# Gated product kept in PSUM and split from there; GpSimd's weight split runs without waiting for VectorE

## The reference

```
h = layernorm(x) * (1 + cb) + sb                      # 2048 x 128
probs = sigmoid(h @ router_w.T + expert_bias)          # 160 experts
top 8 of each token, normalised and scaled by 2.5 -> combine (2048 x 160)
h1 = silu(einsum('th,eih->eti', h, w_gate))            # every expert, 64 inner features
routed = einsum('eti,ehi->th', h1 * combine.T[:, :, None], w_down)
shared = silu(h @ w_gate_shared.T) @ w_down_shared.T
x = x + gb * (routed + shared)
```

## Time and profile before

| | |
|---|---|
| median of 3 runs | 525.52 us (522.47 to 527.17) |
| profiled execution | 521.39 us, span 519.6 us |
| PE busy | 495.6 us, 95% of the span |
| DVE busy | 431.3 us, 83% |
| ACT busy | 392.2 us, 75% |
| POOL busy | 150.6 us, 29% |
| DMA | 110.15 MB, mean 212 GB/s |

### The profile page before, as it was taken

One profiled execution on the slowest core, in us unless ns is written; L12 is line 12 of the kernel. 1 busy time (PEld: TensorE's weight loads), 2 busy tenths in 40 slices (PEclk: granted clock), 3 DMA queues, 4 the chain that ended last, 5 costly groups with the idle time before them and its releaser, 6 DMA issues.

```text
span 519.6 us, 7819 instructions
## 1 busy us (share of the span) xinstructions
PE 495.6 (95%) x2159; PEld 396.0 (76%) x2159; DVE 431.3 (83%) x513; ACT 392.2 (75%) x440; POOL 150.6 (29%) x144
## 2 busy tenths in 40 slices
PE   7686699999999999999999999999999999999996
PEld 5475488777787788888888788788888888888885
DVE  5999888787878788787888797887878888788886
ACT  3267687787878787888888787878878787878873
POOL 3787434222222222222222222222222222222210
PEclk9699899999999999999999999999999999999999
DMA  7000899999999999999999999999999999999962
GB/s 240 1 1 8 216 226 265 227 225 226 234 227 233 242 236 240 230 235 239 230 239 231 221 241 233 232 245 234 237 236 239 242 239 244 233 239 231 225 176 81
DMA packets 38934, 110.15 MB, mean 212 GB/s; under 512 B 6564, under 2 KB 10788, under 8 KB 38920
## 3 DMA queue, kind: packets, MB, share of 16 engines
q1 hardware_dynamic: 38596, 109.32, 88.5%
q10 hardware_dynamic: 324, 0.67, 0.4%
HBM read 107.58 MB, written 2.38 MB: 212 GB/s over the span
## 4 chain that ended last, share of the span: by engine, by line
PE 74%; DMA 13%; DVE 8%; SPq 2%; issue 1%; ACT 1%; POOL 0%; DVEq 0%
PE ps L921 37%; PE ps L906 37%; DMA cb<-combine_scratch 10%; DVE gu L722 2%; DMA combine_scratch<-combT_b 1%; DMA x_sb<-x 1%; DVE stT L686 1%; SPq L280 1%; DVE picked L715 1%; DVE bn L600 1%; DVE picked L703 0%; PE ps L860 0%; DVE mod_gate L659 0%; DVE xn L615 0%; DVE top L698 0%
## 5 line engine op out<-in xcount | busy, mean ns | idle before, releaser
L722 DVE TENSOR_TENSOR gu<-ps,cb 128x1024 f32<-128x1024 f32 x161 | 196.7, 1222 | 76.8 <-DMA cb<-combine_scratch 69.3
L509 ACT ACTIVATE ps<-ps 128x1024 f32<-128x1024 f32 x161 | 162.1, 1008 | 62.8 <-PE ps L906 60.1
L729 DVE TENSOR_TENSOR g_lo<-gu,g_hi 128x1024 fp32r<-128x1024 f32 x162 | 199.8, 1233 | 0.1
L522 ACT ACTIVATE g_hi<-gu 128x1024 fp32r<-128x1024 f32 x162 | 170.9, 1055 | 29.2 <-DVE gu L722 24.7
L404 POOL TENSOR_TENSOR w_lo<-w_raw,w_hi 128x384 fp32r<-128x384 f32 x98 | 99.7, 1017 | 312.1 <-DVE g_lo L729 312.1
L906 PE MATMUL ps<-h_hi,w_hi 128*128 128x512 f32 x324 | 103.8, 401 | 4.1 <-DVE gu L722 1.7
L906 PE MATMUL ps<-h_hi,w_lo 128*128 128x512 f32 x324 | 102.1, 396 | 0.0
L906 PE MATMUL ps<-h_lo,w_hi 128*128 128x512 f32 x324 | 102.1, 396 | 0.0
L921 PE MATMUL ps<-g_lo,w_hi 128*128 128x512 f32 x324 | 100.6, 392 | 1.5 <-DVE g_lo L729 1.5
L921 PE MATMUL ps<-g_hi,w_hi 128*128 128x512 f32 x324 | 101.1, 393 | 0.0
L921 PE MATMUL ps<-g_hi,w_lo 128*128 128x512 f32 x324 | 101.0, 392 | 0.0
(11 more groups left out here) (99 smaller groups left out, 206.9 us busy)
## 6 DMA issues: line engine op xcount, KB each, us to landing
cb<-combine_scratch SPq DMA_DIRECT2D x322, 256.0 KB, 5.1
w_raw<-experts SPq DMA_DIRECT2D x54, 384.0 KB, 7.0
x_sb<-x SPq DMA_DIRECT2D x4, 256.0 KB, 4.9
out<-xn SPq DMA_DIRECT2D x3, 256.0 KB, 2.2
combine_scratch<-combT_a ACTq DMA_DIRECT2D x1, 512.0 KB, 5.5
wmod_sb<-wmod SPq DMA_DIRECT2D x1, 384.0 KB, 3.5
combine_scratch<-combT_a SPq DMA_DIRECT2D x1, 384.0 KB, 3.1
proj_sb<-proj SPq DMA_DIRECT2D x1, 272.0 KB, 4.9
```

The lines of the kernel that those rows point to most:

```text
L509: act.activation(slot(z), slot(z), ACT.Silu).then_inc(silu_done, 1)
L522: act.activation(g_hi[:, k % RING, :], gu[:, k % RING, :], ACT.Copy).then_inc(hi_ready, 1)
L722: dve.tensor_tensor(gu[:, k % RING, :].rearrange("p (b n) -> p b n", b=2), slot(z), cb[:, k % RING, :].rearrange("p (b n) -> p b n", b=2), ...
L729: dve.tensor_tensor(g_lo[:, k % RING, :], gu[:, k % RING, :], g_hi[:, k % RING, :].bitcast(F32), ALU.subtract).then_inc(lo_ready, 1)
```

## The change

gu is gone. The gate writes its product back to the PSUM slot that it reads; hi and lo read the slot. The shared expert's sigmoid, which stood in gu, now stands in cb's first buffer. Since lo is now the last reader of a slot, PE's waits before it overwrites a slot are for lo instead of the gate, in the opening and in the loops. The gate's wait for lo(j-3) is gone. POOL's two halves of w_lo no longer wait for lo.

```diff
                 pool.wait_ge(w_hi_ready, group - FIRST_GROUPS + 1)
-                pair = WG * (group - 2) + 1
                 half = WG * P
                 for n in range(2):
-                    pool.wait_ge(lo_ready, pair + n + 1)
                     cols = slice(n * half, (n + 1) * half)
...
-            def gated_hi(j, k):
+            def gated_hi(j, z, k):
                 act.wait_ge(gated, j + 1)
                 if not (isinstance(j, int) and j < RING):
                     act.wait_ge(down_done, j - RING + 1)
-                act.activation(g_hi[:, k % RING, :], gu[:, k % RING, :], ACT.Copy).then_inc(hi_ready, 1)
+                act.activation(g_hi[:, k % RING, :].rearrange("p (b n) -> p b n", b=2), slot(z), ACT.Copy
+                               ).then_inc(hi_ready, 1)
...
             def gate(j, z, k):
                 dve.wait_ge(silu_done, j + 1)
-                if not (isinstance(j, int) and j < RING):
-                    dve.wait_ge(lo_ready, j - RING + 1)
-                dve.tensor_tensor(gu[:, k % RING, :].rearrange("p (b n) -> p b n", b=2), slot(z),
-                                  cb[:, k % RING, :].rearrange("p (b n) -> p b n", b=2),
+                dve.tensor_tensor(slot(z), slot(z), cb[:, k % RING, :].rearrange("p (b n) -> p b n", b=2),
                                   ALU.mult).then_inc(gated, 1)
...
-            def gated_lo(j, k):
+            def gated_lo(j, z, k):
 
                 dve.wait_ge(hi_ready, j + 1)
-                dve.tensor_tensor(g_lo[:, k % RING, :], gu[:, k % RING, :], g_hi[:, k % RING, :].bitcast(F32),
+                dve.tensor_tensor(g_lo[:, k % RING, :].rearrange("p (b n) -> p b n", b=2), slot(z),
+                                  g_hi[:, k % RING, :].bitcast(F32).rearrange("p (b n) -> p b n", b=2),
                                   ALU.subtract).then_inc(lo_ready, 1)
...
                 users = [p for p in range(j) if FIRST_SLOTS[p] == z]
                 if users:
-                    pe.wait_ge(gated, users[-1] + 1)
+                    pe.wait_ge(lo_ready, users[-1] + 1)
...
                 j = PAIRS * c + BODY * i + k
-                pe.wait_ge(gated, j + 1)
+                pe.wait_ge(lo_ready, j + 1)
                 if ahead % WG == 0:
                     pe.wait_ge(w_split, WGROUPS * c + WG * i + ahead // WG + 1)
```

More of the change, by code:

```diff
@@ L148, in adaln_layer @@
         w_lo = sb("w_lo", [P, RING, 2 * WG * P], F32R)
-        gu = sb("gu", [P, RING, CHUNK])
         g_hi = sb("g_hi", [P, RING, CHUNK], F32R)
@@ L514, in shared_sigmoid @@
                 act.wait_ge(z_ready, 1)
-                act.activation(gu[:, 0, :].rearrange("p (b n) -> p b n", b=2), slot(FIRST_SLOTS[0]), ACT.Sigmoid
+                act.activation(cb[:, 0, :].rearrange("p (b n) -> p b n", b=2), slot(FIRST_SLOTS[0]), ACT.Sigmoid
                                ).then_inc(silu_done, 1)
-            def gated_hi(j, k):
+            def gated_hi(j, z, k):
                 act.wait_ge(gated, j + 1)
@@ L546, in first_hi @@
             def first_hi(j):
-                gated_hi(j, j)
+                gated_hi(j, FIRST_SLOTS[j], j)
             for stage, n in (
@@ L568, in turn @@
                         silu(j + 1, (k + 1) % RING)
-                    gated_hi(j, k)
+                    gated_hi(j, k % RING, k)
                     if k % WG == 1 and not (last and c == CHUNKS - 1 and k > 1):
@@ L734, in shared_gate @@
                 dve.wait_ge(silu_done, 1)
-                both = gu[:, 0, :].rearrange("p (b n) -> p b n", b=2)
-                dve.tensor_tensor(both, slot(FIRST_SLOTS[0]), both, ALU.mult).then_inc(gated, 1)
+                z = slot(FIRST_SLOTS[0])
+                dve.tensor_tensor(z, z, cb[:, 0, :].rearrange("p (b n) -> p b n", b=2), ALU.mult).then_inc(gated, 1)
             def first_gate(j):
@@ L742, in first_lo @@
             def first_lo(j):
-                gated_lo(j, j)
+                gated_lo(j, FIRST_SLOTS[j], j)
             for stage, n in (
@@ L767, in turn @@
                         gate(j + 1, ahead % RING, ahead)
-                    gated_lo(j, k)
+                    gated_lo(j, k % RING, k)
             for c in range(CHUNKS):
```

## The result

| | before | after |
|---|---|---|
| median | 526.35 us (4 runs, 522.47 to 529.44) | 541.76 us (4 runs, 538.88 to 542.84) |
| ratio | | 1.029, 95% interval 1.021 to 1.037 |
| profiled execution, span | 521.39, 519.6 | 542.84, 541.0 |

The change makes the kernel 15.4 us slower by the medians. A ratio leaves out runs that lie over 1.5% above the fastest run of their kernel; a median keeps them. The two profiled executions lie 21.45 us apart: the one of before is shorter than its four runs in the table, and the one of after is the longest of its four. Sizes read from the pair of profiles therefore add up to some 6 us more than the medians show.

The account below looks back on a forecast made before the run. PE was taken as full at 2.78 us a pair, with DMA's limit almost coinciding. 12.95 + 1.4 + 1.4 = +15.7 us on the profiled 521.4 gave 537.1, plus 4.1 to the median 541; range 532 to 550.

Parts of the forecast that it names:

- (e): Two-slot opening: waiting for lo makes a pair cost 5.2 us, not 2.5; +16.1 at pair 14, +12.95 kept.
- (g): Hand-over between token halves: ACT's copy of the first half's sum delays lo(82), and PE now pays +1.4 us.
- (h): Opening: PE's idling before inner(6) and inner(7) brings the half clock; one inner counted, +1.4 us (0 to 4.2).
- (f): Full ring of three slots: 0.50 us in hand, so 0; +1.9 us for late transfers if (e) were nothing.
- 2.3 us of cover: Loops before: PE asks for lo(j) some 2.3 us after inner(j+3) starts, so a late transfer hardly reaches PE.
- (a): DVE: gate(j) no longer waits for lo(j-3), which stands ahead of it in DVE's own order anyway: 0.
- (d): hi reads PSUM, 0.045 us less on ACT, which has room; gate writes PSUM, nothing taken: 0.
- rival 3: DVE writes PSUM slowly: at 0.6 us more per gate, +15 us on top, 556 us; chance 0.09.
- (b): GpSimd's w_lo no longer waits for lo: 0, with -4.8 us (PE's waits for w_split) kept for the range.
- (c): lo reads one SBUF operand instead of two, 1.22 us each; 2.1 us of DVE time hidden under PE: 0.
- rival 2: GpSimd and DVE stop holding each other up and PE never sees the new wait: -6.4 us, 519 us; chance 0.04.
- Rival 1: Transfers pace the opening as now, only the lost cover and the hand-over count: +3.3 us, 529 us; chance 0.08.

Follow-up runs that it names:

- w1_opening: Kernel before with only PE's waits in the opening moved from the gate to lo: 540.98 us, ratio 1.032.
- hybrid: Changed kernel with pairs 0 to 8 put back to the old way (product in gu, PE waits for the gate): 525.84 us, ratio 1.003.
- half_after: Changed kernel with each transfer of combine weights cut to 512 tokens, second half weighted wrongly: 536.88 us, ratio 1.025.
- clock_kept: Changed kernel with eight matmuls of zeros ahead of each wait before inner(5), inner(6), inner(7) and inner(9): 537.88 us, ratio 1.028.
- w2_ring: Kernel before with only PE's wait in the loops moved from the gate to lo: 525.90 us, ratio 1.005.
- w3_both: Kernel before with PE's waits in both opening and loops moved from the gate to lo, nothing else: 543.79 us, ratio 1.037.
- p2_pool_waits: Changed kernel with GpSimd's two waits for lo put back: 539.92 us, ratio 1.030.
- p1_pool: Kernel before with GpSimd's two waits for lo taken out: 524.66 us, ratio 1.001.

## Why the prediction was right

**The mechanism** was right: PE's wait moved to lo, the two-slot opening carries the loss, and every engine is about as fast as before. **The sum** gave +15.7 and 541; measured +15.4 and 541.8. That they agree to within 0.3 us is luck: the interval of the ratio allows some 11 to 19 us, and two errors of about 5 us nearly cancel (see below). Term by term:

- (e), the opening: +16.1 at pair 14 and the clock's 1.4 on top make 17.5; the profile shows 18.2, of which 0.8 us were there before the expert stage's first wait (inner(0) starts that much later). The two-slot pair without extra work on ACT, inner(5) to inner(6), takes 5.23 us where the links gave 5.2. At pair 33 predicted 14.35, measured 15.03. The single starts hold too: inner(6) 79.6 and 79.80, inner(7) 86.4 and 87.14, inner(10) 96.9 (98.3 with the clock) and 98.98. The chain of links from the end of before's trace carried over to the opening unchanged. w1_opening and hybrid show that this wait carries the loss, all but the 2 to 3 us of the ring and the hand-over.
- (g), the hand-over: +1.4, measured 1.42, and the same in half_after.
- (h), the clock: three stretches at 0.50 came in the opening, at inner(2), inner(6) and inner(7). The first was in the working; of the others I counted one at 1.4, and clock_kept puts both together at 1.8, since they covered each inner only in part. PE had idled 2.69 us before inner(6) and 2.74 before inner(7), where the prediction had about 3 and 4.
- (f), the ring: predicted 0, because the opening would put PE behind the transfers. In the profile it is +4.8, so this term was mis-sized there. The step that failed is "(e) gives more than that, so 0 again": the lead lasts only while the transfers keep pace. It was used up at pair 77, where PE first waits for a lo behind a late transfer (0.17 us before inner(80)), and when the rate fell to 222 and 225 GB/s in 360:390 and 390:420 PE paid. So "PE full from pair 14" held up to pair 77 only. Alone (w2_ring) the wait costs 2.6 us by the ratio, the hand-over included, where "if (e) were nothing" had 1.9 + 1.4 = 3.3.
- How much a typical run of the changed kernel loses there stays open. From inner(85) to inner(161), the profiles with the ring's wait for lo lose against before 4.9 us (the changed kernel), 4.7 (w3_both), 3.3 (clock_kept), 1.5 (p2_pool_waits) and 0.1 (hybrid). w1_opening, whose loops wait for the gate as before, loses 1.5. So this loss varies between executions, and a part of it can come without the ring's wait.
- Why the total is still so close to +15.4: the sum took the profile of before, shorter than its runs in the table, and added the 4.1 us up to the median, while the profile of after is its longest run. The two errors, +4.8 for (f) in the profile and the spread of the runs, nearly cancel. That is luck.
- The 2.3 us of cover are right, but the words for them aren't: from the start of inner(j+3) to the last third of down(j) PE goes through three inner thirds and two down thirds, five times 0.46 us.
- (a) and (d): gate into PSUM takes 1.232 against 1.222, lo 1.215; rival 3 is out, far below its 0.44.
- (b) and (c): 0, by p1_pool and p2_pool_waits. The sentence that lo and w_lo hold each other up, and the rule of the Trainium skill beside it ("SBUF — State Buffer", "Who interferes with whom"), hold: 1404 and 1502 ns with two SBUF inputs, 1215 and 1016 with one. The rule's consequence for the time, rival 2, didn't come, since PE, not DVE, sets the pace. In the opening, the two instructions that took 4.00 us took 2.60.
- The estimate of 0.065 us more for a PSUM source, from the Trainium skill's "VectorE: DVE Perf Modes", section on the TRN2 errata, didn't come either: lo became 0.018 us shorter.

**Rival 1** (transfers pace the opening) is out by half_after and by w1_opening; its +3.3 us is about what the ring's wait costs alone.

## What to carry to other kernels

When a buffer is done away with by keeping data in the place it came from, look for who overwrites that place: the buffer was also what let the producer run on. Write the new chain out (here 1.7 + 1.1 + 1.14 + 1.22 + 0.06 = 5.2 us) in each stage of the program, not only in the loop, and count the pairs that it spans. DVE does gate(j+1) before lo(j), so the chain starts at inner(j+1) and ends at the inner that takes the slot of pair j. With three slots that is inner(j+3), two pairs later: 5.56 us at PE's pace, and the chain fits with 0.4 us in hand. With two slots it is inner(j+2), one pair later: each pair takes 5.2 us instead of 2.78. And when a wait is taken away, ask whether its engine is the bound: DVE could lose 27.6 us to contention here without a trace in the time.

## What the runs showed of the hardware

- One transfer whose outer dimension has 2 elements (two rows, each repeated over 64 partitions) ran at 62 GB/s over the span and kept 16.6% of the DMA engines busy, against 212 GB/s and 88.5% for the same bytes in two transfers. The time went from 524 to 1776 us.
- With each 128x3 KB transfer cut into three of 128x1 KB, the profiled execution moved 215 GB/s in 100:270, with the DMA engines full (1.06), where the kernel before moved 234 (0.99). It was one of that kernel's longest runs, so the size is not that of a typical one; by the ratio the kernel became 1.5% slower.
- A DVE subtraction of 128x1024 with both inputs in SBUF took 1.404 us instead of 1.233 on average when GpSimd's subtractions ran beside it, and these 1.502 instead of 1.017. With one input in PSUM neither changed (1.215 and 1.016).
- Eight matmuls that add zeros, ahead of a wait, kept the granted clock at 1.00 through waits after which it had been 0.50 (80.60:83.80 above).
